# Left one-hots of 128 instead of 125 columns in the adjacency-building matmuls of a two-layer graph network

## The reference

```python
def _mp_layer(x, src, dst, edge_attr, W, b):
    loops = jnp.arange(n)                      # zero edge_attr
    msg = jnp.concatenate([x[dst2], x[src2], ea2], axis=1) @ W + b
    return jax.nn.relu(jax.ops.segment_sum(msg, dst2, num_segments=n))
h = relu(_mp_layer(x, src, dst, edge_attr, W1, b1))      # 64 -> 128
out = log_softmax(_mp_layer(h, src, dst, edge_attr, W2, b2), axis=1)   # 128 -> 64
return _layernorm(x + out, axis=-1)
```

## Time and profile before

| what | us |
|---|---|
| median of 3 runs | 251.34 |
| the runs | 251.25, 251.34, 252.3 |
| span of the profiled execution | 251.8 |
| PE busy / PEld busy | 202.7 / 183.9 |
| DVE / POOL / ACT busy | 180.2 / 165.0 / 115.1 |

### The profile page before, as it was taken

The page is one execution under the profiler, slowest core; times in us unless marked ns, Lnnn a source line. Parts: engine busy times, 40 slices in busy tenths (PEclk is TensorE's granted clock), DMA queues, the critical chain, the costliest instruction groups (busy, mean ns, idle before and its releaser), DMA issues.

```text
span 251.8 us, 5544 instructions
## 1 busy us (share of the span) xinstructions
PE 202.7 (81%) x2089; PEld 183.9 (73%) x2089; DVE 180.2 (72%) x436; ACT 115.1 (46%) x235; POOL 165.0 (66%) x338
## 2 busy tenths in 40 slices
PE   1001269599998999989999899989999999999940
PEld 0000159489887898879888798878888999999930
DVE  4035999979876899768977789768410285899881
ACT  2020173267766676757766776667741010101110
POOL 5728998619999999999999999999846000000000
PEclk9999999779999999999999999999999999999995
DMA  1543200000000000000000000000000001010000
GB/s 35 136 115 85 63 21 21 0 3 1 3 2 3 0 3 3 1 3 1 3 1 3 0 3 0 4 0 5 0 3 0 3 3 31 3 31 23 19 15 18
DMA packets 12578, 4.18 MB, mean 17 GB/s; under 512 B 11911, under 2 KB 12126, under 8 KB 12551
## 3 DMA queue, kind: packets, MB, share of 16 engines
q1 hardware_dynamic: 10711, 1.77, 4.0%
q0 software_dynamic: 1840, 2.04, 3.0%
HBM read 2.98 MB, written 0.81 MB: 15 GB/s over the span
## 4 chain that ended last, share of the span: by engine, by line
PE 42%; POOL 34%; DVE 12%; DMA 5%; issue 4%; ACT 1%; POOLq 0%; ACTq 0%; DVEq 0%
PE pset L834 21%; PE acc L826 9%; PE pset L801 5%; POOL u L378 4%; POOL deg L377 4%; DMA adj<-in_dst,adj 4%; POOL t L390 3%; DVE ohl L504 3%; POOL t L394 3%; POOL z L389 3%; POOL u L381 3%; POOL zr L392 3%; POOL base L400 2%; POOL z L398 2%; POOL z L396 2%
## 5 line engine op out<-in xcount | busy, mean ns | idle before, releaser
L715 ACT ACTIVATE adj<-pset 125x1000 bf16<-125x1000 f32 x75 | 77.3, 1032 | 7.0 <-PE pset L801 7.0
L826 PE MATMUL acc<-x,adj 125*125 125x195 bf16 x625 | 75.7, 260 | 2.2 <-POOL x L329 2.2
L504 DVE TENSOR_TENSOR ohl<-iota,keyl 128x1000 bf16<-128x1000 bf16 (+1 forms) x75 | 60.0, 800 | 12.6 <-PE dense L814 11.8
L801 PE MATMUL pset<-ohr,ohl 128*125 128x125 bf16 x600 | 60.0, 255 | 6.0 <-DVE ohr L504 6.0
L826 PEld LDWEIGHTS acc<-x,adj 125*125 125x125 bf16 x625 | 59.7, 143 | 5.7 <-POOL x L329 2.4
L504 DVE TENSOR_TENSOR ohr<-iota,keyr 128x1000 bf16<-128x1000 bf16 (+1 forms) x75 | 60.7, 810 | 0.0
L801 PEld LDWEIGHTS pset<-ohr,ohl 128*125 128x125 bf16 x600 | 50.8, 154 | 7.9 <-DVE ohr L504 6.3
L834 PE MATMUL pset<-z,adj 125*125 125x192 bf16 x625 | 52.8, 247 | 0.0
L834 PEld LDWEIGHTS pset<-z,adj 125*125 125x125 bf16 x625 | 51.7, 136 | 0.3
L529 DVE TENSOR_REDUCE s_sum<-acc 125x65 f32<-125x195 f32 x25 | 9.1, 363 | 19.1 <-PE acc L826 18.7
L751 ACT ACTIVATE x<-x 125x192 f32<-125x192 f32 (+2 forms) x6 | 2.6, 427 | 38.5 <-DVE x L586 38.5
(11 more groups left out here) (114 smaller groups left out, 271.0 us busy)
## 6 DMA issues: line engine op xcount, KB each, us to landing
x_nat<-in_x SPq DMA_DIRECT2D x1, 781.2 KB
out<-x SPq DMA_DIRECT2D x2, 187.5 KB
out<-x SPq DMA_DIRECT2D x3, 93.8 KB
out<-x SPq DMA_DIRECT2D x1, 125.0 KB
adj<-in_dst,adj POOLq DMA_INDIRECT x5, 7.1
adj<-in_edges,adj POOLq DMA_INDIRECT x5, 4.0
adj<-in_edge_attr,adj POOLq DMA_INDIRECT x5, 3.5
se_scratch<-adj SPq DMA_DIRECT2D x5, 2.4 KB
```

The source lines that it names most:

```text
L504: ins = dve.tensor_tensor(out=oh[s][:, :, :, :], in0=iota2[:, 0:Q, :].unsqueeze(1).broadcast_to([128, n, Q, 2]), in1=key[:, g, k0:k0 + 2 * ...
L715: act.activation(adj4[0:Q, g, :, w0:w0 + 8 * WD].rearrange("p h (b e) -> p b h e", b=2), pset[s][0:Q, :, 0:4 * WD * G].rearrange("p b (h e ...
L801: ins = pe.matmul(pset[s][0:Q, i // 4, 0:4 * WD * G].rearrange("p (h e) -> p h e", h=G)[:, :, i % 4 * WD:(i % 4 + 1) * WD], ohl[s][:, i // ...
L826: ins = pe.matmul(acc[0:Q, 0:XW], adj4[0:Q, g, h, :], x3[:, h, :], start=(h == 0), stop=(h == G - 1))
```

## The change

The left one-hots get 128 columns (SLOTS) where they had 125 (Q): their tiles, the comparison that writes them and the PSUM rows that the matmul writes. The right one-hots keep 125 columns. The evacuations still read rows 0 to 124, so the three added columns are computed and not used.

```diff
-        ohl = [sb(f"ohl{s}", [128, 5 if s == 0 else 4, Q, 2], BF16) for s in range(3)]
+        ohl = [sb(f"ohl{s}", [128, 5 if s == 0 else 4, SLOTS, 2], BF16) for s in range(3)]
...
-                for oh, key in ((ohl, keyl), (ohr, keyr)):
+                for oh, key, width in ((ohl, keyl, SLOTS), (ohr, keyr, Q)):
                     ins = dve.tensor_tensor(
                         out=oh[s][:, :, :, :],
-                        in0=iota2[:, 0:Q, :].unsqueeze(1).broadcast_to([128, n, Q, 2]),
+                        in0=iota2[:, 0:width, :].unsqueeze(1).broadcast_to([128, n, width, 2]),
                         in1=key[:, g, k0:k0 + 2 * n].rearrange("p (q o k) -> p q o k", o=1, k=2)
-                        .broadcast_to([128, n, Q, 2]),
+                        .broadcast_to([128, n, width, 2]),
                         op=ALU.is_equal)
...
-                        pset[s][0:Q, i // 4, 0:4 * WD * G].rearrange("p (h e) -> p h e", h=G)[:, :, i % 4 * WD:(i % 4 + 1) * WD],
+                        pset[s][:, i // 4, 0:4 * WD * G].rearrange("p (h e) -> p h e", h=G)[:, :, i % 4 * WD:(i % 4 + 1) * WD],
                         ohl[s][:, i // 2, :, i % 2], ohr[s][:, i // 2, :, i % 2], start=True, stop=True)
...
-                pe.matmul(dense[0:Q, 0:G * WD], ohl[0][:, 4, :, 0], ohr[0][:, 4, :, 0], start=True, stop=True)\
+                pe.matmul(dense[:, 0:G * WD], ohl[0][:, 4, :, 0], ohr[0][:, 4, :, 0], start=True, stop=True)\
```

## The result

The changed kernel is slower. Over 12 runs each the medians are 253.08 us and 251.28 us; the ratio, changed to before, is 1.0051 with a 95% interval of 1.0033 to 1.0068. By the ratio that is 1.3 us more on 251.3; the plain difference of the medians is 1.8 us. The forecast was 249.4 us with a range of 246.5 to 252.2.

A forecast was written before the change was run, and what follows sets the result against it. The prediction took the chain to alternate between GpSimd and TensorE, with TensorE alone at the end. TensorE's -2.6 us and VectorE's +0.7 us gave -1.9 us, so 251.34 became 249.4 us, range 246.5 to 252.2.

The forecast's parts named there:

- What bounds the kernel: Chain of waits passes through TensorE (42%) and GpSimd (34%); both about 96% busy from 56 to 172 us.
- TensorE: Adjacency builds (L801): 128-column loads cut the distance from 69 to 54 ns; -2.6 us on the chain.
- the 15 ns above the streaming floor: Builds start 69 ns apart where streaming 125 columns needs 54; the rest was put down to the stationary operand's load.
- 2.3 us at full clock: Gain from nineteen sets of eight builds on the chain, 0.12 us per set.
- 0.3 us at half clock: Gain from two sets of eight builds on the chain at half clock, 20 ns per build.
- VectorE: Left one-hots grow 13 to 17 ns each, 1.1 us over 25 groups; +0.7 us of it exposed.
- C: Rival: the interleaved step keeps the load slow; no gain, +0.7 us, 252.0 us; chance 0.08.
- D: Rival: the short load at L801 cannot run beside the matmul before it; 255.5, up to 264.6 us; chance 0.07.
- A: Rival: GpSimd, slowed by longer one-hots, refills every wait from 56 to 168 us; -1.4 and +1.1 us, 251.0; chance 0.25.
- The base: Median time of the kernel before from which the forecast subtracts: 251.34 us, 0.5 us below the profiled span.

The follow-up runs named there:

- e3: Changed kernel, but each build writes its 125 columns to PSUM in one run, repair path off; ratio to before 1.0102, cycle 29.36 to 29.45 us.
- f1: Kernel before, with GpSimd's copy of z to bf16 moved to ScalarE; ratio 0.9931, five-group cycle 28.55 us.
- h2: f1 with the product of z and the degree also moved to ScalarE, plus the change; ratio to before 0.9969, cycle 29.0 us.
- f3: f1 with each build writing 125 PSUM columns in one run, reordered by ScalarE's copy, 125-column loads; ratio to before 1.0012.
- f4: f3 with the change, so 128-column loads; ratio to before 1.0056, cycles 29.2 to 29.5 us.
- e1: Changed kernel, left one-hots still written 128 wide but TensorE loads 125 columns; ratio to before 1.0039, cycle 29.45 us.
- e2: Changed kernel, left one-hots loaded 128 wide but VectorE writes 125, last three columns zeroed once; ratio to before 1.0014, cycle 29.27 us.
- f2: f1 with the change; ratio to before 0.996, cycle 29.0 us, only the first cycle 28.51 us.
- g1: Kernel before, unchanged, run once more as one of the compared kernels; ratio 1.0009, cycle 29.19 us, span 251.8 us.

## Why the prediction was wrong

**What bounds the kernel: half right.** In the kernel as it stands a faster TensorE wins little in the middle, as e3 shows. But I took GpSimd's full queue for the reason. f1 gave 0.65 us per cycle where that reason would give 0.9 to 1.7, and h2 pays for the change although GpSimd has room: the engines are tied by the order at L381.

**TensorE: this step failed.** I wrote that the 15 ns above the streaming floor "must be the load of the stationary operand". The load fell by 45 ns, and the distance stayed at 69 ns in two of three sets; in the third only the first distance fell, by 44 ns per group where 24 x 15 = 360 were forecast. I had ruled out streaming by the rate of layer 2, but layer 2 writes 192 columns in one run and a build writes 25 runs of 5; that difference stood in L801's own text, and I listed the load as the only other cause. e3 puts 9 of the 15 ns on the PSUM pattern. The remaining 6 ns are not shown to be the load: f3 and f4 differ by 0.75 ns. With that term gone, nearly all of the 2.3 us at full clock are gone. The 0.3 us at half clock did not come either: the changed kernel's set at 47.67 us has its builds 126 ns apart, as the set at 48.75 us before.

**VectorE: right sign, half the size.** Of the +0.7 us, 0.6 were for the middle; measured are 1.4 us, of which e1 alone gives 0.26 x 4 = 1.0. The size of one operation was about right (the rows above have 0.81 us for 1250 elements and 0.82 to 0.83 for 1280). What failed is that the delays were added up along the chain. They don't add, they tip an order: 10 to 130 ns of head start decide over 0.6 us on GpSimd and about 0.5 us of a group. And the short load works against itself: it brings L814, and with it VectorE's one-hot, forward. In an ordinary group L381 leads the one-hot by 130 ns in the kernel before (at 86.89 us), by 118 in e1, by 90 in e2 and by 77 in the changed kernel. Most of the lost lead is the load's, though e2's own cost is only 0.08 us.

**The rivals.** The measured 253.08 us lies between C (252.0) and D (255.5). C had the right sign and outcome (no gain, VectorE's price exposed), at half the size, though its mechanism was wrong, for the interleaved step doesn't keep the load slow. A named the right engine and cost, 1.1 us exposed, but still credited TensorE with 1.4 us. Had A been joined to "no gain on TensorE", it would have given 252.4, still 0.6 short. D did not happen: a short load does run beside the matmul. All of the chance for faster hung on one cause that I had inferred by exclusion.

**The base** was no fault: 251.34 against 251.28 us.

## What to carry to other kernels

When the distance between matmuls exceeds the streaming time, compare all that differs from the matmul whose rate is used, the output's pattern too, before the load is blamed. Where two engines' operations exclude each other, look for places where they start within 0.1 us of each other and the later one is waited for: an edit of a few nanoseconds elsewhere can flip them, and an explicit wait can fix the order. Such a wait has a price of its own; here it cost less than it won back (0.36 us per cycle). Compare repeated cycles within traces when the effect is smaller than the scatter of the runs.

## What the runs showed of the hardware that was not expected

- Builds of 125 columns: 67 to 74 ns apart when they write PSUM in 25 runs of 5 floats (before, changed), 57 to 62 ns when in one run (e3, f3, f4). A 128-column load takes 109 ns instead of 154, also with a step of two elements, and changes neither, but for the first distance behind the short matmul L907 (71 ns instead of 115).
- ScalarE's copy of 1000 columns takes 1339 ns (f3) instead of 1032 (before) when it writes SBUF in runs of 5 bf16 elements instead of 20; it reads PSUM in runs of 125 there. Which side costs was not tested apart.
- GpSimd's product L381 takes 0.29 us when it starts ahead of VectorE's one-hot and 0.88 to 0.96 us when it starts 20 to 100 ns behind it (before, changed, f2, h2).
- One program has its stretch at half clock at different places: it came at 46.6 us in one execution of the kernel before and at 57.6 us in another (g1). The second's first cycle took 32.12 us instead of 29.20; in it lie a wait of 1.7 us for u and, behind it, 3.4 us at half clock.
